# A four-layer mixer and routed feed-forward on one core: the mixer's work dealt anew among the engines, in a new order

## What is computed

```python
def mixer(h, Wi, cw, cb, dtb, Alog, Dh, gw, Wo):      # one layer
    z, xBC, dt = split(h @ Wi)                         # 256, 256 + 128 + 128, 8 columns
    xs, Bm, Cm = split(silu(cb + causal_conv4(xBC, cw)))
    dt = softplus(dt + dtb)
    dA = exp(dt * -exp(Alog))
    # for each token: state = state * dA + (dt * x) B;  y = state . C
    y = scan(...) + Dh * xs
    return rmsnorm(y * silu(z), gw) @ Wo
for l in range(4):
    h = h + mixer(rmsnorm(h, block_norm_w[l]), ...)
```

## Time and profile before

| | |
|---|---|
| median of three runs | 1139.5 us |
| the profiled execution | 1144.4 us |
| its span, first to last instruction | 1142.4 us |
| mean granted TensorE clock | 0.951 |
| mixer, the first to the last sum onto `h` | 92 to 792 us |
| rest (routing, experts, return) | 792 to 1142 us |
| busy in the whole span: PE, DVE, ACT, POOL | 87%, 85%, 76%, 59% |

### The profile page before, as it was taken

One profiled execution on the slowest core, in us unless ns is written; L12 is line 12 of the kernel. 1 busy time (PEld: TensorE's weight loads), 2 busy tenths in 40 slices (PEclk: granted clock), 3 DMA queues, 4 the chain that ended last, 5 costly groups with the idle time before them and its releaser, 6 DMA issues.

```text
span 1142.4 us, 20674 instructions
## 1 busy us (share of the span) xinstructions
PE 995.8 (87%) x6136; PEld 557.6 (49%) x6136; DVE 970.0 (85%) x1801; ACT 864.6 (76%) x1636; POOL 675.6 (59%) x853
## 2 busy tenths in 40 slices
PE   5699999999999999999999999985878767999970
PEld 4244454445445444554454455432444436777750
DVE  6679999999999999999999999974788766888865
ACT  4679999899989999999899999983566534556540
POOL 0167767767776777577557656752354451666660
PEclk9789999999999999999999999997889888999995
DMA  5000232223112321100000000000010016766638
GB/s 144 16 12 12 70 133 76 74 75 133 67 68 103 114 72 69 60 3 4 16 10 3 3 5 3 3 3 0 20 38 27 31 38 202 236 227 218 218 114 220
DMA packets 57420, 83.91 MB, mean 73 GB/s; under 512 B 17562, under 2 KB 37664, under 8 KB 57312
## 3 DMA queue, kind: packets, MB, share of 16 engines
q1 hardware_dynamic: 52320, 74.13, 20.3%
q0 software_dynamic: 4992, 8.48, 2.2%
HBM read 44.99 MB, written 37.83 MB: 72 GB/s over the span
## 4 chain that ended last, share of the span: by engine, by line
POOL 40%; issue 28%; PE 18%; DVE 7%; ACT 3%; DMA 2%; SPq 1%; POOLq 1%; DVEq 0%; ACTq 0%
POOL own L1637 6%; POOL dtx L1611 6%; POOL yt L1660 5%; POOL xw L1616 5%; POOL y L1664 5%; PE bank L662 2%; PE bank L663 2%; PE bank L664 2%; POOL WS L1648 2%; PE bank L674 2%; PE bank L676 2%; PE bank L673 2%; POOL h L1652 2%; POOL WS L1646 1%; POOL dt_ L1603 1%
## 5 line engine op out<-in xcount | busy, mean ns | idle before, releaser
L1335 DVE SCALAR_TENSOR_TENSOR cv<-bank,PAR,cv 128x511 f32<-128x511 f32 (+2 forms) x384 | 273.9, 740 | 6.5 <-ACT cv L942 2.8
L1351 DVE SCALAR_TENSOR_TENSOR M<-E,bank 128x512 f32<-128x512 f32 x256 | 168.0, 676 | 21.5 <-ACT E L930 16.1
L1660 POOL TENSOR_TENSOR yt<-yt,ti 128x384 f32<-128x384 f32 x64 | 64.1, 1001 | 194.7 <-DVE ti L1451 194.7
L930 ACT ACTIVATE E<-bank 128x512 f32<-128x512 f32 x256 | 149.0, 596 | 19.1 <-DVE M L1351 18.2
L475 PE MATMUL bank<-hn,WA 128*128 128x512 f32 x256 | 144.6, 647 | 20.7 <-DVE cv L1335 20.2
L1691 POOL DMA_INDIRECT RS<-y,XR x92 | 98.8, 1074 | 78.6 <-DVE y L1548 55.3
L1684 POOL DMA_INDIRECT XS<-stage,IDX x64 | 65.5, 1024 | 79.0 <-DVE run L1310 62.0
L1082 ACT ACTIVATE hr<-bank,W1B 128x512 f32<-128x512 f32 x92 | 63.4, 689 | 56.8 <-PE bank L664 48.9
L543 PE MATMUL bank<-M,dtx 128*32 128x128 f32 x2048 | 82.9, 279 | 14.6 <-DVE o_sb L1370 14.2
L1478 DVE TENSOR_TENSOR hL<-hr,hH 128x512 fp32r<-128x512 f32 x124 | 87.1, 703 | 4.3
L1664 POOL TENSOR_TENSOR y<-yt,zs 128x512 f32<-128x512 f32 x64 | 81.4, 1272 | 5.0
(11 more groups left out here) (244 smaller groups left out, 2610.5 us busy)
## 6 DMA issues: line engine op xcount, KB each, us to landing
XS<-PADT SPq DMA_DIRECT2D x32, 520.0 KB, 4.8
W1B<-WD SPq DMA_DIRECT2D x23, 514.0 KB
W2B<-WD SPq DMA_DIRECT2D x23, 512.5 KB
WD<-WS SPq DMA_DIRECT2D x16, 512.0 KB, 2.9
XR<-XS SPq DMA_DIRECT2D x23, 260.0 KB
RW<-w_in SPq DMA_DIRECT2D x18, 256.0 KB, 4.7
xin<-x_in SPq DMA_DIRECT2D x4, 512.0 KB, 8.3
PC<-p SPq DMA_DIRECT2D x128, 6.0 KB
```

The source lines that it names most:

```text
L930: f(E[i % 2][:, :], bank[2 + i % 2][:, :], ACT.Exp).then_inc(e_a, 1)
L1335: stt(out=cv[t][:, s:L], in0=src[:, 0:L - s], scalar=PAR[:, bass.ds(cw + 3 - s, 1)], in1=cv[t][:, s:L], op0=ALU.mult, op1=ALU.add).then_in ...
L1351: stt(out=M[i % 4][:, :].rearrange("p (n t) -> p n t", n=4), in0=E[i % 2][:, :].rearrange("p (n t) -> p n t", n=4), scalar=1.0, in1=bank[5 ...
L1660: tt(yt[t][:, 128:512], yt[t][:, 128:512], ti[t][:, :], ALU.add).then_inc(fin_p, 1)
```

## The change

Four things change in the mixer, and the order of every `body`.

- The squares of y's two halves are summed by POOL (`sum_squares`), and PE makes their mean with one product in place of two.
- The gate's first half is taken by silu straight from bank 0 (`gate_silu(0)`), without `zraw`. What used bank 0 after it moves: the mean for the next norm goes to bank 6 and early in the step (`square_mean_of_next`), the turned step sizes go to bank 3 (`turn_steps`), the third state to bank 2.
- The norm's product `hn` is made by POOL, as h times `rB` only, into two buffers in turn. The layer's norm weight is multiplied into the six projection weights once per layer (`scale_weights`, POOL, from `WA_raw` to `WA`) and into the step-size weights once at the start. The weights are loaded to `WA_raw` in the third step of a layer.
- ACT squares `h` for the norm two steps ahead (`norm_square(k + 2)`), at the end of the step.

The core of the diff:

```diff
                 def square_mean():
-                    wait(pe, sq_a, 2 * (i2 + 1))
+                    wait(pe, sum_p, i2 + 1)
+                    if N:
+                        wait(pe, rb_a, 2 * k + 3)
...
-                    mm(bank[6][:, :], mean256[:, :], sqy[0][:, :], start=True, stop=False)
-                    mm(bank[6][:, :], mean256[:, :], sqy[1][:, :], start=False, stop=True).then_inc(ss_mm, 1)
+                    mm(bank[6][:, :], mean256[:, :], sqy[0][:, :], start=True, stop=True).then_inc(ss_mm, 1)
+                def square_mean_of_next():
+                    wait(pe, sqh_a, k + 2)
+                    if B:
+                        wait(pe, t_ev, 4 * j + 2)
+                    mm(bank[6][:, :], mean128[:, :], sqh[:, :], start=True, stop=True).then_inc(ms_mm, 1)
+                def turn_steps():
+                    wait(pe, dtc_v, 2 * k + 2)
+                    wait(pe, step_p, 2 * k + 2)
+                    if B:
+                        wait(pe, e_a, 8 * j + 8)
+                    nc.tensor.transpose(bank[3][:, 0:P], dt_[:, :], ident)
...
+                def project_next(t):
+                    wait(pe, silu_a, 6 * k + 1 + t)
+                    project_early(k + 1, t)
+                def from_states(t):
+                    wait(pe, s_v, 5 * j + 5)
+                    if A and t == 1:
+                        wait(pe, dta_a, 5 * k + 5)
+                    wait(pe, e_a, 8 * j + 7 + t)
...
+                def gate_silu(t):
+                    wait(act, fin_p, 4 * (k - 1))
+                    wait(act, pj_mm, 6 * k + 5 + t)
+                    f(zs[:, bass.ds((k % 2) * 2 * L + t * L, L)], bank[t][:, :], ACT.Silu).then_inc(silu_a, 1)
...
-                    stt(out=hn[:, :], in0=h[:, bass.ds(n % NB * L, L)], scalar=PAR[:, bass.ds(n // NB * NPAR + C_BNW, 1)],
-                    in1=rB[:, :], op0=ALU.mult, op1=ALU.mult).then_inc(hn_v, 1)
...
+            def norm_apply(n):
+                wait(pool, rb_a, 2 * n + 2)
+                wait(pool, pj_mm, 6 * (n - 1))
+                wait(pool, dt_mm, n - 1)
+                tt(hn[n % 2][:, :], h[:, n % NB * L:(n % NB + 1) * L], rB[:, :], ALU.mult).then_inc(hn_p, 1)
+            def scale_weights(layer, t):
+                wait(pool, wa[t], 16 * (layer + 1))
+                wait(pool, pj_mm, 6 * (NB * layer - 1) + t + 1)
+                norm_weight = PAR[:, layer * NPAR + C_BNW:layer * NPAR + C_BNW + 1].to_broadcast([P, P])
+                tt(WA[t][:, :], WA_raw[t][:, :], norm_weight, ALU.mult).then_inc(wa_p, 1)
+                def sum_squares():
+                    wait(pool, sq_a, 2 * (i2 + 1))
+                    tt(sqy[0][:, :], sqy[0][:, :], sqy[1][:, :], ALU.add).then_inc(sum_p, 1)
...
-                if N and (k + 1) % NB == 0:
-                    for t in range(5):
-                        next_projection(t)
+                if k % NB == 2 and k // NB + 1 < NL:
+                    layer = k // NB + 1
+                    for t in range(6):
+                        wait(sp, wa_p, 6 * (layer - 1) + t + 1)
+                        sp.dma_start(WA_raw[t][:, :], rows(w_in, (6 * layer + t) * P * P, P)).then_inc(wa[t], 16)
```

More of the change, by code:

```diff
@@ new lines, in body @@
+                if A:
+                    step_sizes()
+                if B and not A:
+                    pe.wait_ge(s_ffw, 16)
+                if B:
+                    products()
+                    decays(0)
+                    turn(0)
+                    turn(1)
+                    turn(2)
+                if B and not A:
+                    mean(0)
+                if N:
+                    square_mean_of_next()
+                if B:
+                    decays(1)
+                if A:
+                    project(2)
@@ L835, in norm_log @@
                 wait(act, ms_mm, n + 1)
-                f(lnm[:, :], bank[0][:, :], ACT.Ln, bias=eps5).then_inc(rb_a, 1)
+                f(lnm[:, :], bank[0 if n == 0 else 6][:, :], ACT.Ln, bias=eps5).then_inc(rb_a, 1)
             def norm_root(n):
                 wait(act, rb_a, 2 * n + 1)
-                wait(act, hn_v, n)
+                wait(act, hn_p, n)
                 f(rB[:, :], lnm[:, :], ACT.Exp, scale=-0.5).then_inc(rb_a, 1)
@@ L980, in body @@
-                if C and not B:
-                    square_h(1)
-                if A:
-                    wait(act, step_p, 2 * k + 1)
-                    f(dA[:, :], dt_[:, :], ACT.Copy, scale=PAR[:, bass.ds(pk + C_NA, 1)]).then_inc(da_a, 1)
-                if B:
-                    decay_exp(2)
-                    turned(3)
-                if A:
-                    tap(2)
-                if B:
-                    decay_exp(3)
-                if B and not A:
-                    square_x(0)
@@ new lines, in body @@
+                nc.scalar.preload_act_table_set(EXPLN)
+                if B and not A:
+                    root_h(0)
+                if A:
+                    size_bias()
+                if B:
+                    decay_exp(0)
+                    turned(0)
+                    turned(1)
+                    decay_exp(1)
+                if A:
+                    size_exp()
+                    size_log()
+                if C:
+                    square_y(0)
+                if B:
+                    turned(2)
@@ L1036, in body @@
+                if C:
+                    square_y(1)
                 if N:
                     norm_log(k + 1)
+                if A:
+                    size_rate()
+                    tap(2)
                 if B:
[L1039 removed]
+                    decay_exp(2)
+                    decay_exp(3)
                 if N:
                     norm_root(k + 1)
[L1042 to L1043 removed]
+                if C and not B:
+                    square_h(1)
@@ new lines, in body @@
+                if A:
+                    to_end()
+                if C:
+                    log_y()
+                if B and not A:
+                    square_x(0)
+                if B:
+                    chunk_exp()
+                if C:
+                    root_y()
+                if B:
+                    turned(3)
+                if A:
+                    tap(3)
+                if C and not B:
+                    root_h(1)
+                    square_x(1)
+                if B and not A:
+                    root_x(0)
@@ new lines, in body @@
+                if B:
+                    row_exp(0)
+                if A and not N:
+                    square_h(0)
+                if B:
+                    decay_exp(4)
+                    decay_exp(5)
+                if B and not A:
+                    square_m(0)
+                if B:
+                    row_exp(1)
+                    decay_exp(6)
+                    decay_exp(7)
+                if A:
+                    gate_silu(0)
+                if B and j % NB == 0:
+                    scale_output_weights()
@@ L1044, in body @@
+                if k + 2 < STEPS:
+                    norm_square(k + 2)
                 if B and not A:
                     root_m(0)
+                if A:
+                    gate_silu(1)
+                if B and not A:
                     halve(0)
@@ L1403, in body @@
                     add_mamba(1)
+                if A:
+                    tap(2, 3)
+                if C and not B:
                     centre(1)
@@ L1459, in _ @@
-            norm_apply(0)
+                    state_add(3)
+                    skip_sum(0)
+                    skip_sum(1)
+                if B and not A:
+                    scale(0)
+                if B:
+                    carried(0)
+                if B and not A:
+                    halve(0)
+                if B:
+                    carried(1)
             dve.wait_ge(s_cst, 16)
@@ new lines, in body @@
+                if B:
+                    by_step(0)
+                if C and not B:
+                    sum_squares()
+                if A:
+                    step_size()
+                if N and (k + 1) % NB == 0:
+                    scale_weights((k + 1) // NB, 0)
+                if B and C:
+                    sum_squares()
+                if B:
+                    to_chunk_end(0)
+                    by_step(1)
+                if N and (k + 1) % NB == 0:
+                    scale_weights((k + 1) // NB, 1)
```

413 lines of the change are left out of this document (194 added, 219 removed).

## The result

The changed kernel takes 1109.05 us (median of four runs, 1107.96 to 1113.82) against 1139.51 us (1137.28 to 1142.09) for the kernel before: a ratio of 0.974, with a 95% interval of 0.9704 to 0.9776. The forecast was 1110, with 1088 to 1130.

A forecast was written before the change was run, and what follows sets the result against it. A loop through PE, DVE and ACT, none full, was taken to bound the 22.57 us step. Terms -27 - 3.5 + 2 = -28.5 us gave 1116 profiled, 1111 as median, stated as 1110; range 1088 to 1130.

The forecast's parts named there:

- 27 us for the steps: Mixer loop: step falls from 22.57 to 21.7 us, 0.87 saved some 31 times.
- 3.5 for the first one: First step: gate silu 0 and the early projection follow projection 4 at once, four silus remain: 3.5 us less.
- 2 back for the layers' weights: Steps 7, 15 and 23: six POOL weight products, 2.8 us; the first two also split weights, losing 2 us in all.
- The contention: DVE instructions reading two SBUF tensors, or the small `spend`, stand until POOL's current instruction ends; 0.5 us a step taken beyond 21.2.
- The bound of 3.6 us: Upper bound on DVE's delay behind POOL at decays and `spend`: 1.14 twice (`own`) plus 1.28 (h + o).
- the first wait: DVE, before the carried parts: waits 0.3 us for PE's `from_states(0)`.
- the rival without contention: POOL's `own_rows` end before the state decays, so no contention counts: step 21.1, 1092 us; chance 0.25.
- PE loses one of two 512-column matmuls: PE's mean of y's squares: one product against mean256 fewer, about 0.86 us; PE's work 21.59 to 20.7 us a step.
- the first step of the argument: Chain taps, projection 4, `zraw`, mean, `lnm`, last exponential is cut: mean moves to bank 6 and the step's start.
- POOL sets the step: In some sixteen steps with splits POOL's 19.4 us plus waits nears 20.5: step 22.2, 1126 us; chance 0.13.
- The port eats it all: State decays and `spend` all wait for long POOL instructions; decides from 1.75 us a step; at 2.6, 1166 us; chance 0.08.
- No effect: PE and ACT are as full as DVE, saved `hn` returns as a longer exponential wait: 1139 us; chance 0.04.

The follow-up runs named there:

- the run without splits: Changed kernel with POOL halving expert weights in full only in steps 1 to 3, 8 columns instead of 512 in steps 4 to 18: 1107.39 us, ratio 0.9709.
- the early square: Changed kernel with ACT's square of h for the norm two steps ahead moved from between the gate silus to ahead of decay_exp(6): 1103.4 us, ratio 0.9666.
- the first decay freed: Changed kernel with the first state decay reading the first state from PSUM (bank 4) instead of its SBUF copy: 1106.32 us, ratio 0.9688.
- the run with three edits: Changed kernel with first decay reading PSUM, ACT's square ahead of decay_exp(6), and scale_out behind tap(2, 3) on DVE: 1128.7 us, ratio 0.9906.
- the run with two edits: Changed kernel with the first state decay reading PSUM and ACT's square moved ahead of decay_exp(6): 1098.95 us, ratio 0.9635.

## Why the prediction was right

**The size.** Forecast: 27 us for the steps, 3.5 for the first one, 2 back for the layers' weights. Measured in the profiles: 27.3 between the first and the last sum onto h, the layers' steps included; the second step's first tap starts at 47.90 instead of 51.29 us, 3.4. The first two steps together gave 7.3, 2 more than I had counted, by the clock of one step in the profile before (see the result). That is why the profiled executions differ by 36.3 us and not by the 28.5 of the sum, while the medians differ by 30.5. The pitch was forecast as 21.7 and is 21.65.

The 2 us for the layers are right as a sum, in part by luck. Steps 7 and 8 together take 43.5 us where their neighbours take 43.2, and so do 15 and 16: 0.3 each for the weights' products on POOL, and none around step 23. Another 0.4 to 0.6 comes in steps 9 and 10, and again in 17 and 18 and in 25 and 26, where ACT multiplies a layer's output weights (`scale_output_weights`, 0.58 us in steps 9, 17 and 25). This the prediction doesn't name. The kernel before does the same work and keeps its 22.57 there.

**DVE's account.** Per step, from the two group views and the timelines: `hn` 0.75 less; waits 1.0 before, 0.31 before `o_sb` and 0.05 elsewhere after, 0.64 less; standing behind POOL 2 x (861 - 425) + (548 - 400) - (805 - 622) = 0.84 more. One term I had not named: the new order puts other work between a copy and the instruction that needs it. From the copy of the first state to the next start it is 0.34 us (519.79 to 520.13) instead of 0.53 (502.93 to 503.46), and 0.2 us less behind the causal mask: 0.39 less. Together -0.75 - 0.64 + 0.84 - 0.39 = -0.94, against the 0.92 that the pitch fell. This is where DVE's time went; which of it sets the step is another matter.

**The contention** came where and as large as laid out: 0.9 us for the first decay and 1.5 for both in a split step had been estimated; 1.01 - 0.42 = 0.6 and (1.14 + 0.81) - 0.84 = 1.1 were measured. The bound of 3.6 us was far off, for the reason given: what stands moves to the next gap. (One of the readings behind it is a little wrong: the running sum of the earlier trace rows ends 0.28 us after `dtx`, not 0.4. The decay above ends 0.28 us after `own`, just so.) That it is contention is shown by the decay that reads PSUM. The Trainium skill (SBUF — State Buffer, SBUF: two separate sides) says that DVE stands with two SBUF inputs, against a GpSimd instruction that reads SBUF; the 412 and 1124 ns of that run agree.

**What was luck.** The 21.7 is DVE's list, 20.82, with 0.3 for a wait and 0.5 for contention and shifts. The contention was there, but the pitch does not rest on it: without it on the first decay the mean pitch is 21.64 instead of 21.65, and shorter decays in the split steps did no more. In the steps without a split the chain from the last exponential through ACT, PE's mean and the root of y to `o_sb` holds the pitch, at 21.56; shortened by one square, it gives 21.33. The prediction had laid this chain out and put its wait at 0.1 to 0.4 us, "which partly swallows the first wait, not adds to it". It is nearly as long as DVE's list with contention, and so the number came out. For the same reason the rival without contention was wrong about its 21.1.

**What was wrong in it.** Of the step "PE loses one of two 512-column matmuls" I had said only that PE's list is 20.7 us and fits. It isn't PE's list that counts but where the product stands: between the squares and the root for which DVE waits. Undone, it costs 0.59 us a step, more than hn's 0.49. And the first step of the argument, that the new order cuts the chain that held the kernel before, is true but not enough: alone it brought 0.3%. The forecast was made with both moves in place, so it didn't depend on what each was worth. The wait of 0.3 us for PE before the carried parts didn't show; the decays' delay covers it, and it came out (0.64) when that was gone.

**The rivals.** No contention: refuted by the decays. POOL sets the step: refuted by the run without splits. (Against it the prediction set POOL's wait of 6.4 us before `finish_y`, which is that of a step without a split; with one it was 5.30, and is 1.30.) The port eats it all: no; it takes 0.84 us of DVE's time a step, half of the 1.75 from which it would have decided. No effect: no.

What stays open: in the split steps the two chains are within 0.1 us of each other. With the early square DVE does not wait before `o_sb` and the pitch is 21.51; with the first decay freed it waits, and the pitch is 21.59. In the changed kernel it waits in 9 of these 16 steps, 0.3 to 0.5 us. Their mean pitch is 21.69, with the decay freed 21.64, with the early square 21.59, with both 21.41; in the steps without a split the four are 21.59, 21.63, 21.36 and 21.36. And what holds the 21.33 of most steps in the last of these was not tested.

## What to carry to other kernels

When three engines are each over 90% busy, a move of work and a new order are worth little one by one: here 0.3% for the order, and a loss of 0.4% and 1.5% for either move in the old order, but 2.6% for all. Read for each freed microsecond which wait it will join, and for each product which later instruction of the fullest engine hangs on it. Work moved from VectorE to GpSimd comes back in part at those VectorE instructions that read two SBUF tensors; one operand from PSUM avoids that (1.02 us became 0.41), but it gives time only where that engine's list sets the step: alone it moved the pitch by 0.01 us here, and in the split steps, behind a shorter second chain, by 0.18.

## What the runs showed of the hardware beyond that

The granted clock of TensorE can fall within a full mixer step. In the run with three edits it is 1.00 from 540 to 545 us, 0.67 as a mean from 545 to 550, and 0.99 after: a stretch of 3.4 us, from 546.7, at the lower of its two levels, 1.2 GHz. A group of 16 products of `within` took 0.64 us before it and 1.08 within it, and the two of projection 4 took 1.72 us instead of 1.13. ACT waits 2.61 us for the last decays, where it waits 1.15 in the step before, and the step takes 23.54 us instead of 21.93. In the changed kernel the mean clock from 92 to 600 us is 1.00.

Ahead of the fall PE had waited 0.31 us and then 0.85 us, with a single short product between. Five of the 28 steps from 98 to 722 us have a fall, three of them of 3.4 us (a step of 23.5) and two of 6.8 (25.2), and each begins 1 to 2 us behind the longer wait. But these waits are not enough: 0.30 and 0.77 us stand at the same place in the steps of 21.93 us, in which the clock stays at 1.00, and ahead of the fall at 413.6 us they are 0.30 and 0.77 as well. What decides in which step it falls is not shown, and no run removes the waits and keeps the rest. Of the 29.0 us between the spans of this run and of the run with two edits, the longer waits at full clock make some 0.6 us a step, and the falls 11 in all.
